# A three-stage network on one core: keys by values in 32-column blocks, one gate transpose, two value groups per four heads, halves of the hidden tile freed one by one

## The reference

```python
# block 0, attention (cosformer, 16 heads of 8), in float32
q, k = relu(xn @ Wq.T + bq), relu(xn @ Wk.T + bk);  v = xn @ Wv.T + bv
q_, k_ = concat(q*sin, q*cos), concat(k*sin, k*cos)        # sin, cos of the position
kv = einsum('nld,nlm->ndm', k_, v)                         # per head 16 x 8
z = 1 / maximum(q_ . sum_l k_, 1e-4);  attn = (q_ @ kv) * z;  out = attn @ Wo.T + bo
# block 0, ffn: 2 shared + 16 routed experts of 64, top 4 of a softmax as gates
act = gelu(xn @ up);  routed act is multiplied by its gate;  y = act @ down
# block 1, attention: rope, causal softmax, 16 heads of 8
weights = softmax(Q @ K.T / sqrt(128) + causal mask);  out = (weights @ V) @ ow
# block 1, ffn: 8 experts, each token goes to the best one
h = xn @ w1[e];  a, g = split(h);  y = p[e] * ((silu(a) * g) @ w2[e])
```

## Time and profile before

| | |
|---|---|
| median of 3 runs | 1342.65 us (1342.58 to 1343.49) |
| the profiled execution | 1337.22 us, span 1335.4 us |
| PE busy | 1201.5 us (90%) |
| DVE, ACT, POOL busy | 962.6, 945.2, 682.3 us |
| mean granted TensorE clock | 0.961 of full |
| DMA | 101.46 MB, mean 76 GB/s |

### The profile page before, as it was taken

One profiled execution on the slowest core, in us unless ns is written; L12 is line 12 of the kernel. 1 busy time (PEld: TensorE's weight loads), 2 busy tenths in 40 slices (PEclk: granted clock), 3 DMA queues, 4 the chain that ended last, 5 costly groups with the idle time before them and its releaser, 6 DMA issues.

```text
span 1335.4 us, 28936 instructions
## 1 busy us (share of the span) xinstructions
PE 1201.5 (90%) x9960; PEld 696.8 (52%) x9960; DVE 962.6 (72%) x2450; ACT 945.2 (71%) x1312; POOL 682.3 (51%) x933
## 2 busy tenths in 40 slices
PE   5877989989999999999999999999987878779996
PEld 3433343444454544545454545545433556679996
DVE  5437585888888988888888888888768553346664
ACT  3224777868797888888897888888765646546663
POOL 3452536464847566574847575574854212323333
PEclk9887999999999999999999999999986988999998
DMA  4650505141433416061532325060734311112222
GB/s 142 157 116 21 106 15 112 37 102 40 99 77 57 104 31 127 7 129 30 109 69 65 95 40 122 12 128 15 157 123 94 98 29 29 39 45 72 72 70 45
DMA packets 85502, 101.46 MB, mean 76 GB/s; under 512 B 11734, under 2 KB 63062, under 8 KB 85096
## 3 DMA queue, kind: packets, MB, share of 16 engines
q1 hardware_dynamic: 77904, 86.44, 28.9%
q0 software_dynamic: 7456, 13.19, 3.5%
HBM read 73.68 MB, written 25.90 MB: 75 GB/s over the span
## 4 chain that ended last, share of the span: by engine, by line
PE 72%; ACT 10%; DVE 8%; issue 5%; POOL 5%; DMA 0%; ACTq 0%; DVEq 0%; POOLq 0%
PE PS L734 10%; PE PS L701 10%; PE PS L537 9%; PE PS L585 8%; PE PS L668 6%; PE PS L686 5%; PE PS L516 4%; PE PS L745 4%; ACT flow L846 3%; ACT qp L837 3%; PE PS L529 3%; PE PS L551 2%; POOL early L1258 2%; PE PS L652 2%; PE PS L718 1%
## 5 line engine op out<-in xcount | busy, mean ns | idle before, releaser
L846 ACT ACTIVATE flow<-PS 128x1024 f32<-128x1024 f32 x320 | 320.3, 1023 | 93.8 <-PE PS L686 90.0
L1271 POOL TENSOR_SCALAR_AFFINE_SELECT flow<-flow 128x256 f32<-128x256 f32 (+1 forms) x448 | 191.3, 442 | 301.1 <-ACT flow L846 299.6
L701 PE MATMUL PS<-flow 128*32 128x512 f32 (+3 forms) x2048 | 181.1, 455 | 3.8 <-POOL flow L1271 2.3
L1101 DVE TENSOR_REDUCE nm<-PS 128x2 f32<-128x1024 f32 x128 | 154.6, 1218 | 38.7 <-PE PS L652 38.7
L1258 POOL TENSOR_TENSOR early<-early 128x512 f32<-128x512 f32 x128 | 164.7, 1303 | 3.0 <-DMA early<-gate_rows 2.5
L837 ACT COPY qp<-PS 2x512 f16<-2x512 f16 x256 | 147.5, 576 | 18.6 <-PE PS L676 15.0
L1304 POOL DMA_INDIRECT out_y<-ysb,rowu x72 | 70.9, 985 | 169.4 <-DVE rowu L1209 162.4
L585 PE MATMUL PS<-early,down 128*128 128x512 f32 x288 | 150.4, 626 | 6.3 <-POOL early L1258 5.0
L537 PE MATMUL PS<-xnT,up 128*128 128x512 f32 x288 | 147.9, 630 | 8.6 <-DVE rb L1045 2.7
L668 PE MATMUL PS<-kp,qp 34*128 34x512 f16 (+3 forms) x1024 | 125.4, 309 | 32.6 <-ACT flow L846 16.4
L1103 DVE TENSOR_REDUCE nm<-PS 128x2 f32<-128x768 f32 x128 | 121.4, 948 | 41.9 <-PE PS L652 40.6
...
...
## 6 DMA issues: line engine op xcount, KB each, us to landing
...
```

The costliest lines, as they stand in the source:

```text
L701: ins = pe.matmul(m.PS[32 * j:32 * j + 32, m.PV, kt * P:], m.vst[b % 2][:, kt, 4 * g + j, :], m.pt[:, r, k * L + o:k * L + o + L - kt * P] ...
L846: act.activation(m.pt[:, n % RING, :], m.PS[:, i:i + 2, :].rearrange("p k c -> p (k c)"), ACT.Exp, scale=1.0 / SCALE).then_inc(s["exp"], 1)
L1101: dve.tensor_reduce(nm[:, 3, :, n], ps, AX_X, ALU.max, negate=True).then_inc(s["max"], 1)
L1271: ins = pool.affine_select(part, part, [[0, part.shape[1]], [1, P]], ALU.is_ge, nothing, base=0, channel_multiplier=-1)
```

## The change

- `kv`: the values are now scaled by sin and cos, not the keys. `kvr` holds the values as four blocks of 32 columns, each followed by a column of ones (`VB` = 132 columns), and DVE writes `vs` from it. ACT takes the Relu of the keys in place (a new stage function `kv`, semaphore `krelu`). PE multiplies each block of 32 keys by its own block of 33 scaled columns for sin and cos together: 16 products with 32 weight columns and 66 moving columns, on four column groups of PE. DVE repeats the 32 columns four times when it masks by `K_BD`.
- `gT`: one transpose of all 64 gate columns; ACT copies 64x128; the DMA to `gate_rows` reorders.
- `value`: two goes per four heads, units 0 and 1, then 2, 3 and 4. The ring `pt` has 6 places.
- `hidden`: the two halves have semaphores of their own (`ha_mm`, `hg_mm`); the first bank is freed by `silu`, the second by `glu`, and PE waits for each before its half. tanh starts after the first half.
- `q` on POOL waits for the `gated` products of the batch before (its tile `qs` moved).
- All places in the order are new. In `OPENING`, batch 0 goes through `down` and rope before batch 1's keys, the fills stand before `q`, and batch 0's relay stands before batch 1's gates on SP. The first 30 tiles have places of their own (`TILES`); 5 of them stand within the attention, so `NBETWEEN` becomes 5.

The diff, cut to its core (of the tables of places, the steady ones and the tiles):

```diff
-KVW = 2 * D + 1 + NR0
+VB = D // 32 * 33
+KVW = D + VB + NR0
...
-RING = 4
+RING = 6
...
-VALUES = {1: (0, 1), 3: (2, 3), 4: (4,)}
+VALUES = {1: (0, 1), 4: (2, 3, 4)}
...
-    return 3 * (n // SL) + (1, 1, 2, 2, 3)[n % SL]
+    return 2 * (n // SL) + (1, 1, 2, 2, 2)[n % SL]
...
@@ -120,142 +121,147 @@
-    stats0=[-58.35],
-    norm0=[-55.95],
-    xnT0=[-51.4],
-    kvr=[-49.45, -46.3, -44.8, -44.05],
-    up=[-42.35, -39.1, -39.1, -38.5, -38.1, -37.5, -37.45, -36.95, -35.45],
-    q=[-48.85],
-    kv=[-41.45],
-    route0=[-41.9],
-    gate=[-41.3],
-    attn0=[-40.8],
-    gT=[-40.35],
-    at0T=[-39.25])
+    stats0=[-57.55],
+    norm0=[-54.5],
+    xnT0=[-50.4],
+    kvr=[-47.7, -44.25, -42.95, -42.35],
+    up=[-39.85, -39.55, -37.7, -37.6, -37.55, -36.05, -35.7, -35.65, -33.65],
+    q=[-49.6],
+    kv=[-39.45],
+    route0=[-41.4],
+    gate=[-39.65],
+    attn0=[-38],
+    gT=[-39],
+    at0T=[-36.4])
 SECOND = placed(
-    down=[-36.05, -35.1, -34.5, -33.7, -33.7, -31.35, -30.6, -29.8, -29.25],
-    gated=[-38.2, -37.65, -36.05, -35.45, -34.15, -32.45, -31.6, -30.85],
-    x1=[-28.25],
-    stats1=[-27.45],
-    norm1=[-25.95],
-    xnT1=[-23.95],
-    rope=[-22.55, -18.75],
-    parts=[-19.3, -17.05],
-    relay=[-13.15],
-    v=[-16.9],
-    logits=[-23],
-    route1=[-22.6],
-    expert=[-19.9],
-    ranks=[-18.8],
-    sort=[-19.65, -18.45, -14.05, -13.1])
+    down=[-34.4, -33.95, -33.5, -32.85, -32.05, -30.05, -29.45, -28.05, -27.95],
+    gated=[-37, -34.5, -33.4, -33.4, -32.25, -31.8, -31.6, -30.1],
+    x1=[-26.5],
+    stats1=[-24.85],
+    norm1=[-23.85],
+    xnT1=[-22.9],
+    rope=[-20.15, -17.45],
+    parts=[-17.85, -15.75],
+    relay=[-11.5],
+    v=[-16.15],
+    logits=[-22.2],
+    route1=[-20.75],
+    expert=[-18.75],
+    ranks=[-16.55],
+    sort=[-17.3, -16.9, -16.7, -12.75])
...
-    score=[0.3, 1.3, 3.5, 7, 8.5, 9.15, 9.6, 10.8, 12.35, 13.1, 13.15, 14.35, 16.45, 16.55, 17.05, 17.05, 18.3, 18.7,
-           19.55, 20.3],
-    max=[-6.75, -5.4, -2.35, -2.3, -1.8, -1.25, 1, 1.3, 1.95, 2.25, 4.75, 4.75, 6, 6.95, 8.25, 8.75, 9.5, 10.25,
-         10.25, 11],
-    mparts=[-1.7, 3.9, 8.9, 12.75],
-    mrows=[-0.85, 8.2, 9.7, 13.6],
-    value=[3.65, 8.9, 11.5, 12.85, 13.95, 14.8, 16.55, 17.85, 17.9, 19.6, 20.4, 21.25],
-    sums=[15.8, 21.5],
-    heads=[16.75, 24.65],
-    mT=[26.1],
-    out=[27.25],
-    sort2=[28.05, 29.75, 29.75, 29.9])
+    score=[2.65, 3.2, 3.75, 6.3, 9.35, 10, 12.85, 12.95, 14.2, 14.25, 16.75, 16.95, 17.15, 17.8, 18.4, 19.25, 19.8,
+           20.6, 21.1, 21.75],
+    max=[-4.2, -4.2, -4.05, -3, 0, 0.5, 1.25, 2.05, 2.7, 3.7, 4, 4.15, 5.1, 6.35, 6.65, 6.7, 8.55, 10.25, 10.7, 11.5],
+    mparts=[0.45, 5.95, 7.3, 11.9],
+    mrows=[1.55, 6.6, 10.45, 15.45],
+    value=[6.15, 13.9, 15.8, 15.9, 19.4, 20.75, 22.25, 23],
+    sums=[16.65, 23.25],
+    heads=[19.05, 23.8],
+    mT=[26.9],
+    out=[29.5],
+    sort2=[31.95, 32.9, 37, 39.15])
...
+TILES = placed(
+    tile=[6, 16.1, 17, 22.85, 26.15, 68.35, 70.05, 93.85, 127.45, 136.6, 146.7, 150.85, 153.75, 168.45, 177.45,
+          186.05, 203.6, 205.65, 216.85, 219, 258.95, 269.2, 270.5, 277.35, 289.6, 311.75, 362.5, 385.55, 395.5, 437.7])
...
-TILE0, STEP = 0, 1.3
+STEP = 1.3
 
 
 def tile(n):
-    return TILE0 + STEP * n
+    if n < 0:
+        return TILES[0][0] + STEP * n
+    return TILES[n][0] if n < len(TILES) else TILES[-1][0] + STEP * (n - len(TILES) + 1)
...
-            work[stage] = [(at, free[at])]
-            free[at] = free[at + 1] = "glu", i + 1
+            work[stage] = [(at, free[at]), (at + 1, free[at + 1])]
+            free[at], free[at + 1] = ("silu", i + 1), ("glu", i + 1)
...
-        pe.wait_ge(s["ks"], NT * (b + 1))
+        pe.wait_ge(s["vs"], NT * (b + 1))
+        pe.wait_ge(s["krelu"], b + 1)
         ps = bank(("kv", b, i))
-        for sc in range(2):
-            for t in range(NT):
-                ins = pe.matmul(ps[:, sc * 256:sc * 256 + D + 1], m.ks[:, t, sc, :], m.kvr[:, t, D:2 * D + 1],
-                                start=(t == 0), stop=(t == NT - 1))
+        for t in range(NT):
+            for j in range(4):
+                rows = slice(32 * j, 32 * j + 32)
+                ins = pe.matmul(ps[rows, 0:66].rearrange("p (s c) -> p s c", s=2), m.kvr[:, t, rows],
+                                m.vs[:, t, :, 33 * j:33 * j + 33], start=(t == 0), stop=(t == NT - 1), skip_group_check=True)
...
-        for t in range(NT):
-            ins = pe.transpose(ps[0:NR0, t * P:(t + 1) * P], m.gate[:, t, :], ident)
-        ins.then_inc(s["gT_mm"], 1)
+        pe.transpose(ps[0:NT * NR0, 0:P], m.gate[:, :, :].rearrange("p t e -> p (t e)"), ident).then_inc(s["gT_mm"], 1)
...
-        bank(("hidden", 0, n))
-        at = work[("hidden", 0, n)][0][0]
-        for i in range(2 * FC):
-            ins = pe.matmul(m.PS[:, at + i // FC, i % FC * P:(i % FC + 1) * P], m.w1s[:, n % WS, i * P:(i + 1) * P],
-                            m.xsT[:, n % 2, :], start=True, stop=True)
-        ins.then_inc(s["h_mm"], 1)
+        for k, done in enumerate(("ha_mm", "hg_mm")):
+            ps = bank(("hidden", 0, n), k)
+            for i in range(FC):
+                ins = pe.matmul(ps[:, i * P:(i + 1) * P], m.w1s[:, n % WS, (k * FC + i) * P:(k * FC + i + 1) * P],
+                                m.xsT[:, n % 2, :], start=True, stop=True)
+            ins.then_inc(s[done], 1)
...
+    def kv(b, i):
+        act.wait_ge(s["kvr"], NT * (b + 1))
+        act.activation(m.kvr[:, :, 0:D], m.kvr[:, :, 0:D], ACT.Relu).then_inc(s["krelu"], 1)
...
-            ins = dve.tensor_scalar(m.ks[:, t, sc, :], m.kvr[:, t, 0:D], 0.0,
-                                    const(m, K_SC)[:, sc * NT + t:sc * NT + t + 1], ALU.max, ALU.mult)
-        ins.then_inc(s["ks"], 1)
+            ins = dve.tensor_scalar(m.vs[:, t, sc, :], m.kvr[:, t, D:D + VB],
+                                    const(m, K_SC)[:, sc * NT + t:sc * NT + t + 1], None, ALU.mult)
+        ins.then_inc(s["vs"], 1)
...
-            dve.tensor_tensor(m.kvm[:, sc, 0:D], ps[:, sc * 256:sc * 256 + D], const(m, K_BD), ALU.mult)
-            ins = dve.tensor_scalar(m.kvm[:, sc, D:], const(m, K_BH), ps[:, sc * 256 + D:sc * 256 + D + 1], None, ALU.mult)
+            block = ps[:, sc * 33:sc * 33 + 32].unsqueeze(1).to_broadcast([P, 4, 32])
+            dve.tensor_tensor(m.kvm[:, sc, 0:D].rearrange("p (j c) -> p j c", j=4), block,
+                              const(m, K_BD).rearrange("p (j c) -> p j c", j=4), ALU.mult)
+            ins = dve.tensor_scalar(m.kvm[:, sc, D:], const(m, K_BH), ps[:, sc * 33 + 32:sc * 33 + 33], None, ALU.mult)
...
+        dve.wait_ge(s["hg_mm"], n + 1)
...
+            pool.wait_ge(s["gated"], (NC - 1) * b)
...
-        sp.dma_start(m.gate_d, m.gT).then_inc(s["d_gate"], 16)
+        sp.dma_start(m.gate_d.rearrange("e (t q) -> t e q", t=NT), m.gT).then_inc(s["d_gate"], 16)
...
+    by_block = lambda w, last: np.concatenate([np.concatenate([w[:, j:j + 32], last], 1) for j in range(0, D, 32)], 1)
```

More of the change, by code:

```diff
@@ new lines @@
+OPENING = [placed(
+    stats0=[-546.05],
+    norm0=[-480.15],
+    xnT0=[-458.8],
+    kvr=[-450.8, -450.75, -449.35, -446.1],
+    up=[-433.8, -427.5, -373.95, -341.85, -324.1, -312.2, -304.45, -245.6, -233.05],
+    q=[-391.55],
+    kv=[-320.6],
+    route0=[-315.3],
+    gate=[-265.9],
+    attn0=[-246.45],
+    gT=[-269.15],
+    at0T=[-244.8],
+    down=[-223.4, -222.4, -221.35, -219.65, -219.35, -219.2, -210.2, -208.35, -198.5],
+    gated=[-365.95, -365.7, -355.5, -351.25, -349.8, -343.9, -335.95, -320.6],
+    x1=[-182],
+    stats1=[-178.4],
+    norm1=[-168.6],
+    xnT1=[-152.05],
+    rope=[-149.1, -144.6],
+    parts=[-148.2, -138.8],
+    relay=[-95.4],
+    v=[-145.25],
+    logits=[-136.85],
+    route1=[-125.4],
+    expert=[-104.1],
+    ranks=[-91.15],
+    sort=[-142.85, -140, -139.15, -130.75],
+    score=[-51.15, -43.15, -38.55, -38, -29.3, -28.25, -27.05, -25.75, -24.2, -21.45, -21.25, -18.45, -14.5, -10.35,
+           -4.3, -2.65, -1.55, 1.1, 1.15, 2.2],
+    max=[-83.55, -83.05, -82.1, -81.7, -79.1, -75.05, -74.95, -73.9, -72, -64.8, -61.15, -56.1, -50.95, -48.85,
+         -46.8, -32.8, -32.7, -29.25, -25.55, -24.4],
+    mparts=[-76.2, -55.95, -37.8, -22.05],
+    mrows=[-72.2, -49.35, -34, -16.1],
+    value=[-32.15, -27.15, -24.75, -15.45, -6.35, -1.85, 0.25, 3.25],
+    sums=[-7.65, 10.35],
+    heads=[1.45, 15.5],
+    mT=[18.05],
+    out=[26.45],
+    sort2=[30.05, 32.05, 36.95, 38.55]), placed(
+    stats0=[-254.05],
+    norm0=[-211.8],
+    xnT0=[-211.1],
+    kvr=[-157.1, -157.05, -151.4, -143.15],
+    up=[-197.35, -184.2, -180.25, -175.15, -171.6, -170.25, -142.55, -140.6, -135.5],
+    q=[-160.9],
+    kv=[-115.45],
+    route0=[-124.65],
+    gate=[-108.65],
+    attn0=[-108.4],
+    gT=[-107.1],
+    at0T=[-102.85],
+    down=[-98.9, -89.15, -84.3, -81.05, -73.2, -70.5, -70.25, -66.4, -63.4],
+    gated=[-149.8, -145.6, -145.05, -142.15, -140.15, -138.35, -128.75, -128.65],
+    x1=[-59.6],
```

(27 more changed lines are left out.)

114 lines of the change are left out of this document (18 added, 96 removed).

## The result

The changed kernel takes 1391.5 us (median of 4 runs, 1383.7 to 1392.7) against 1342.6 us, ratio 1.035 with a 95% interval of 1.032 to 1.039. I had forecast 1295 us: 49 us slower where I had written 48 us faster. The profiled execution took 1383.7 us, 1381.9 of it span.

The account below looks back on a forecast made before the run. PE was taken as the bound in the steady periods (59.11 of 60.49 us busy). Gains of 17 + 26 + 5 = 48 us off the profiled 1337.2 give 1289.2, with 5.4 back to the median 1295 us; 8 in 10: 1268 to 1326.

Parts of the forecast that it names:

- PE at 98% can only gain what it loses in work: Steady periods: PE's saved work shortens them, 1.5 us per batch less 0.3 subtracted; 1.2 x 14 batches, 17 us.
- hidden behind PE: Keys' Relu on ACT: +0.3 us per batch net of the smaller gate copy, hidden while PE is the bound.
- PE's work: PE work per batch: key product 0.8 us less, gates 0.3, values 0.4; sum 1.5 us, ends 0.5 and 2.1.
- the lower end: Key product on PE: 0.65 us if columns set the pace, against 2.0 if records do; 1.2 was taken.
- rival B: Period holds 60 us: key product paced by records (2.0 us), ordering around ACT and DVE; total 1307 us; chance 0.11.
- rival D: Key product pays the 0.21 us column-group entry four times, 0.6 us more per batch; total 1303 us; chance 0.04.
- The ends of 5 and 28 us for the steady part: Lowest and highest gain expected from the steady periods over 14 batches, around the forecast 17 us.
- The gates turned and the value groups: PE, per batch: one gate transpose for four gains 0.3 us; two value groups per four heads for three gain 0.4.
- Rival C: Merged value group waits on PE for an exp and its select, 1.43 us at full; 1375 us; any size 0.07.
- The end: From batch 14's `oT` copy on: 254.3 against 280.1 us, 20 tiles at 2.79 instead of 4.6; 26 us gained.
- Rival A: Last attention, unfilled, drops PE to 1.2 GHz and takes 60 us; end gains 14; total 1307 us; chance 0.15.
- The opening: Up to batch 5's `down` evacuation: of 58 idle PE us, 5 gained (ends: 10 lost, 15 gained).

Follow-up runs that it names:

- after_reduce: Changed kernel with the two small DVE products of the maxima replaced by one reduction, low half of the maxima left out; 1321.4 us.
- reduce_keys: Same as after_reduce, with the keys' Relu on ACT also made its own stage straight behind the last key and value product; 1307.5 us.

## Why the prediction was wrong

- **The step that failed: "PE at 98% can only gain what it loses in work", with 0.3 us taken off for all the rest.** The new order of places was declared not to be priced, and none of the rivals had it make a period longer except through the value groups. It put a 16-column DVE product beside a POOL run of which 5.9 us were still to come, and the product stood through all of it; that is 5.8 us in each of 11 batches, 64 of the 70 us that come back without it. A sign of it could have been read from before: the same line there went from 170 to 1277 ns on one shape. I priced each engine's own work and no collision between engines.
- **The Relu "hidden behind PE", because "`up` products stand between": wrong.** The products stand on PE; what counts is what stands on ACT ahead of the Relu. 0.87 us of waiting in the new order, 1.87 in the old one; taking it away is worth 10 us (ratios 0.981 and 0.973).
- **PE's work: right, and nearly worthless.** Forecast 1.5 us less per batch, measured 1.9 (59.11 to 57.23). The key product takes 0.67 us for 32 records, not 1.2: the lower end, the one paced by columns, was right, and its sum of 4 x 0.11 + 0.2 = 0.65 came within 0.02. With that the record pace in rival B and rival D, an entry paid at every step, are refuted for this product; the entry was paid once at most. But of 1.9 us the period gave back 0.24 before the Relu moved and 0.76 after. Of rival B the period came true (60.25 in after_reduce), and of its two causes the second, "the ordering around ACT and DVE": waits for maxima, exps and the Relu. The ends of 5 and 28 us for the steady part do not follow from 0.5 and 2.1 less 0.3 over 14 batches (3 and 25); nothing here hangs on it.
- **The gates turned and the value groups: right.** One transpose is 0.30 us, groups of 24 records take 1.50. Rival C is refuted: PE's wait for a select in a period is 0.25 us, against 0.86 per group at which it would have decided.
- **The end: right.** 252.5 us from batch 14's anchor against 254.3 forecast, 280.1 before; 27.6 us gained for 26. Rival A fell: 45.65 us at clock 0.85, not 60 at 0.71. PE ran 64 records of the first expert product between the anchors, the four tiles foreseen.
- **The opening: wrong.** Forecast 5 gained. The first mark moved by 13.9, about 11 of it two long products (at 290 and 356 us). Without them it stands at 365.4 in after_reduce and 361.2 in reduce_keys, 6 and 2 later than before.
- **The sum.** Instead of 17 + 26 + 5 gained, the profiled execution lost 54.6 us in nine periods and 13.9 ahead of them, and gained 22.0 behind. These 22.0 are the 27.6 of the end less 5.5 that the stretch from the mark of batch 14 to its anchor grew (157.5 against 152.0 us). Why that stretch grew I did not trace. None of my rivals had the long product's mechanism, and the 0.07 for slower belonged to another one.
